# Layer 1 of a two-layer graph network: the block loop pipelined over three stages, with the edge-feature loads moved from SyncE to ScalarE

## What is computed

```python
h = relu(layernorm(x))
x = x + segment_sum(h[src], dst) @ W_rel.T + b_rel + h @ W_root.T      # layer 0
h = relu(layernorm(x))
w = silu(edge_attr_50 @ We1 + be1) @ We2 + be2                          # [200000, 128]
agg = segment_sum(h[src] * w, dst)                                      # layer 1
x = x + h + silu(agg @ Wn1 + bn1) @ Wn2 + bn2
```

## Time and profile before

| | us |
|---|---|
| median of 3 runs | 5581.96 |
| the profiled execution, whole | 5534.93 |
| its span, first to last instruction | 5533.1 |
| mean granted TensorE clock | 0.623 of full speed |
| POOL, PE, DVE, ACT busy | 54%, 46%, 36%, 21% |

### The profile page before, as it was taken

The page is one execution under the profiler, slowest core; times in us unless marked ns, Lnnn a source line. Parts: engine busy times, 40 slices in busy tenths (PEclk is TensorE's granted clock), DMA queues, the critical chain, the costliest instruction groups (busy, mean ns, idle before and its releaser), DMA issues.

```text
span 5533.1 us, 50710 instructions
## 1 busy us (share of the span) xinstructions
PE 2539.5 (46%) x10946; PEld 1935.5 (35%) x10946; DVE 1975.2 (36%) x6931; ACT 1188.8 (21%) x2730; POOL 2971.4 (54%) x3135
## 2 busy tenths in 40 slices
PE   1333333333333333342555555555555555554456
PEld 1323333333333333331333333444334433333334
DVE  3444444444444444451222332333333333222224
ACT  1333333333333333330010111111111111100001
POOL 6656666666666666625454454554444445445442
PEclk9555555555555555556666666666766666666667
DMA  2111111121211211211111121211111112111111
GB/s 66 51 52 51 51 53 50 52 54 49 56 50 49 55 51 50 57 40 48 51 52 50 50 54 51 54 53 49 51 49 51 51 49 54 51 51 52 51 51 47
DMA packets 205552, 284.71 MB, mean 51 GB/s; under 512 B 67808, under 2 KB 135442, under 8 KB 205298
## 3 DMA queue, kind: packets, MB, share of 16 engines
q0 software_dynamic: 100096, 205.20, 14.3%
q1 hardware_dynamic: 64146, 57.99, 3.9%
q10 hardware_dynamic: 41184, 20.45, 1.3%
HBM read 262.97 MB, written 20.45 MB: 51 GB/s over the span
## 4 chain that ended last, share of the span: by engine, by line
another core or an unknown queue 32%; PE 22%; DVE 20%; issue 19%; DVEq 4%; ACT 3%; DMA 0%; ACTq 0%; POOL 0%; SPq 0%; POOLq 0%
PE seg_a L315 9%; PE seg_b L315 5%; DVE onehot L552 5%; PE ew_ps L359 4%; DVE e_stats L568 3%; PE hid_ps L354 3%; DVE ew_ps L652 3%; DVEq L559 3%; DVE rows L656 2%; ACT rows L410 2%; DVE e_mv L572 2%; DVE agg L563 1%; DVE n_stats L585 1%; DVE e_rstd L577 1%
## 5 line engine op out<-in xcount | busy, mean ns | idle before, releaser
L283 POOL DMA_INDIRECT rows<-h_rows,idx x1564 | 1486.9, 951 | 1608.8 <-DMA idx<-src_cols 696.6
L283 POOL DMA_INDIRECT rows<-x,idx x1564 | 1483.5, 949 | 873.5 <-issue 469.1
L315 PE MATMUL seg_a<-onehot,rows 128*128 128x128 f32 x3312 | 751.4, 398 | 1519.4 <-ACT rows L410 454.8
L315 PEld LDWEIGHTS seg_a<-onehot,rows 128*128 128x128 f32 x3312 | 646.9, 290 | 1766.8 <-issue 1667.4
L315 PE MATMUL seg_b<-onehot,rows 128*128 128x128 f32 x2944 | 614.0, 374 | 1274.2 <-DVE rows L656 516.2
L315 PEld LDWEIGHTS seg_b<-onehot,rows 128*128 128x128 f32 x2944 | 528.9, 270 | 1493.0 <-issue 1298.8
L410 ACT ACTIVATE rows<-rows,e_shift,e_rstd 128x128 f32<-128x128 f32 x1564 | 643.2, 481 | 889.9 <-DVE e_shift L579 699.9
L488 ACT ACTIVATE hidden<-hid_ps,be_col 128x512 f32<-128x512 f32 x391 | 268.6, 687 | 2532.2 <-remote 1228.1
L359 PE MATMUL ew_ps<-we_sb,hidden 128*128 128x128 f32 x3128 | 564.2, 340 | 152.9 <-ACT hidden L488 111.7
L359 PEld LDWEIGHTS ew_ps<-we_sb,hidden 128*128 128x128 f32 x3128 | 524.7, 253 | 190.7 <-ACT hidden L488 142.4
L563 DVE TENSOR_TENSOR agg<-seg_b,agg 128x128 f32 x368 | 107.6, 292 | 1210.4 <-remote 812.6
(11 more groups left out here) (93 smaller groups left out, 898.2 us busy)
## 6 DMA issues: line engine op xcount, KB each, us to landing
rows<-x,idx POOLq DMA_INDIRECT x1564
rows<-h_rows,idx POOLq DMA_INDIRECT x1564
ef_a<-ef_blocks SPq DMA_DIRECT2D x69, 300.0 KB
ef_b<-ef_blocks SPq DMA_DIRECT2D x46, 300.0 KB
xs<-x SPq DMA_DIRECT2D x26, 256.0 KB
y_rows<-ys ACTq DMA_DIRECT2D x26, 256.0 KB
ys<-y_rows SPq DMA_DIRECT2D x26, 256.0 KB
out<-xs ACTq DMA_DIRECT2D x26, 256.0 KB
```

The lines of the kernel that those rows point to most:

```text
L283: pool.indirect_dma_start(out=rows[:, u, t, :], out_offset=None, in_=table, in_offset=bass.IndirectOffsetOnAxis(ap=idx[:, j:j + 1], axis=0 ...
L315: mm = pe.matmul(seg[u % 2][:, 0:P], rows[:, u, t, :], onehot[:, u % 2, t, :], start=(t == 0), stop=(t == TB - 1))
```

## The change

1. Layer 1's block loop is staggered. In step u PE does the first product of u + 2, the second product of u + 1, and the segment sum of u; DVE does the message of u, the one-hot of u + 1, the accumulation of u - 1 and the bias of u + 1. A prologue starts blocks 0 and 1, and at the end of each iteration the streams run on into the next one. After the last iteration two first products and one second product are left over and drained.
2. `hid_ps` and `ew_ps` get two banks each; `node_t` and `node_o` share one bank, for which PE waits (`hold` on `s_mout`) before the node update of layer 1. `onehot` gets three buffers; `hi_row` moves into a part of `agg[1]` to make room.
3. The edge-feature loads leave SP and go into ACT's stream: group g + 2 is issued after the silu of the last block of group g. SP's layer-1 program is then that of layer 0, with `ys` in place of `xs`.

```diff
 SyncE, layer 1
-                    for u in range(U):
-                        g, blocks = u // EF_BLOCKS, min(EF_BLOCKS, U - u)
-                        if u % EF_BLOCKS == 0:
-                            hold(sp, s_hid, done(i, u - EF_BLOCKS - 1) if g else done(i, EF_BLOCKS * (EF_GROUPS - 1) - 1 - U))
-                            sp.dma_start(ef[g % 2][:, 0:blocks, :],
...
-                        if u == HALF + EF_BLOCKS:
-                            for v in range(HALF):
-                                hold(sp, s_rows[1][v], i * (16 * TB) + 16 * TB)
-                            load_idx(it + 1, 0, HALF, s_idx_a)
+                    node_y([loop_group(it)], i)
+                    for u in range(HALF):
+                        hold(sp, s_rows[1][u], i * (16 * TB) + 16 * TB)
+                    load_idx(it + 1, 0, HALF, s_idx_a)
+                    for u in range(HALF, U):
+                        hold(sp, s_rows[1][u], i * (16 * TB) + 16 * TB)
                     load_idx(it + 1, HALF, U, s_idx_b)
 TensorE, layer 1
                 def hidden_layer():
+                    hold(pe, s_mout, n - r + 1)
                     hold(pe, s_acc[1], acc_done)
...
-                    edge_hidden(i, 0)
                     for u in range(U):
-                        edge_weights(i, u)
-                        if u + 1 < U:
-                            edge_hidden(i, u + 1)
                         if u in steps:
                             steps[u]()
-                        pe.wait_ge(s_msg, i * U + u + 1)
-                        segment_sum(1, i, u)
+                        if u + 2 < U:
+                            edge_hidden(i, u + 2)
+                            edge_weights(i, u + 1)
+                        elif u + 1 < U:
+                            edge_weights(i, u + 1)
+                            edge_hidden(i + 1, u + 2 - U)
+                        else:
+                            edge_hidden(i + 1, u + 2 - U)
+                        pe.wait_ge(s_msg, i * U + (u + 1))
+                        segment_sum(1, u)
+                        if u + 1 == U:
+                            edge_weights(i + 1, 0)
 ScalarE, layer 1
+            def load_ef(it, g):
+                first, last = g * EF_BLOCKS, min((g + 1) * EF_BLOCKS, U)
+                act.dma_start(ef[g % 2][:, 0:last - first, :],
...
                     for u in range(U):
-                        act.wait_ge(s_hid, done(i, u))
-                        act.wait_ge(s_ew, slot_free(i, u, 2))
...
+                        edge_silu(i, u)
+                        g = u // EF_BLOCKS
+                        if u == min((g + 1) * EF_BLOCKS, U) - 1:
+                            load_ef(it + (g + 2) // EF_GROUPS, (g + 2) % EF_GROUPS)
 VectorE, layer 1
+                    edge_bias(i, 0)
+                    one_hot(1, it, 0)
                     for u in range(U):
-                        one_hot(1, i, it, u)
                         message(i, u)
-                        add_window(1, i, it, u)
+                        if u + 1 < U:
+                            one_hot(1, it, u + 1)
+                        if u > 0:
+                            add_window(1, i, it, u - 1)
+                        if u + 1 < U:
+                            edge_bias(i, u + 1)
+                        else:
+                            add_window(1, i, it, u)
```

More of the change, by code:

```diff
@@ L29 @@
 EF_BLOCKS = 3
+HOT = 3
 EF_GROUPS = -(-U // EF_BLOCKS)
@@ L110, in build @@
         seg = [bank("seg_a"), bank("seg_b")]
-        hid_ps, ew_ps = bank("hid_ps"), bank("ew_ps")
-        node_t, node_o = [bank("node_t"), hid_ps, ew_ps], [bank("node_o"), *seg]
+        hid_ps, ew_ps = [bank("hid_a"), bank("hid_b")], [bank("ew_a"), bank("ew_b")]
+        node = bank("node")
+        node_t, node_o = [node, hid_ps[0], ew_ps[0]], [node, *seg]
         assert LATE <= 3
@@ L310, in _, with segment_sum @@
             pe.wait_ge(s_ident, 1)
[L312 to L313 removed]
+            def segment_sum(layer, u):
                 for t in range(TB):
[L315 removed]
+                    mm = pe.matmul(seg[u % 2][:, 0:P], rows[:, u, t, :], onehot[:, u % HOT, t, :],
                                    start=(t == 0), stop=(t == TB - 1))
@@ L479, in node_update1, with edge_silu @@
                 return {3: hidden_layer, 9: result, 14: stored}
+            def load_ef(it, g):
+                first, last = g * EF_BLOCKS, min((g + 1) * EF_BLOCKS, U)
+                act.dma_start(ef[g % 2][:, 0:last - first, :],
+                              ef_blocks[bass.ds(it * U + first, last - first)].rearrange("k c e -> c k e")
+                              ).then_inc(s_ef[g % 2], 16)
+            load_ef(0, 0)
+            load_ef(0, 1)
+            def edge_silu(i, u):
+                act.wait_ge(s_hid, i * U + (u + 1))
+                nc.scalar.activation(hidden[:, u % 2, :], hid_ps[u % 2][:, :], ACT.Silu,
+                                     bias=be1_col[:, :]).then_inc(s_silu, 1)
             with act.Fori(0, passes) as p:
@@ L485, in _ @@
                     for u in range(U):
-                        act.wait_ge(s_hid, done(i, u))
-                        act.wait_ge(s_ew, slot_free(i, u, 2))
-                        nc.scalar.activation(hidden[:, u % 2, :], hid_ps[:, :], ACT.Silu,
-                                             bias=be1_col[:, :]).then_inc(s_silu, 1)
+                        edge_silu(i, u)
+                        g = u // EF_BLOCKS
+                        if u == min((g + 1) * EF_BLOCKS, U) - 1:
+                            load_ef(it + (g + 2) // EF_GROUPS, (g + 2) % EF_GROUPS)
                         if u in steps:
                             steps[u]()
+            for g in range(2):
+                hold(act, s_ef[g], passes * (8 * EF_GROUPS * ITERS) + 16)
+            edge_silu(passes * ITERS, 0)
+            edge_silu(passes * ITERS, 1)
+            hold(act, s_ew, passes * ITERS * U + 1)
             with act.Fori(0, n_late) as j:
```

49 lines of the change are left out of this document (25 added, 24 removed).

## The result

The changed kernel takes 4950.97 us (median of 4 runs, 4927.46 to 4962.84); in the same session the kernel before takes 5581.93. The ratio is 0.8861, 95% interval 0.882 to 0.8903. Forecast were 4970 us and a range of 4785 to 5220. The profiled execution is one of 4927.46 us with a span of 4925.0 and a mean clock of 0.638.

A forecast was written before the change was run, and what follows sets the result against it. Bound: POOL's waits, 34.8 us per iteration for row indices. Start 2473, ring full 2573, pause to 2581, 371 blocks at 6.1 to 4844, tail to 4923; the 610 drop off the 5581.96 median gives 4970 us, range 4785 to 5220.

The forecast's parts named there:

- The wait for the index load goes: In layer 1, POOL's wait for the first half's row indices, 34.8 us per iteration, goes.
- Rival three: If node_y or the landing of rows comes late, POOL still waits up to 34.8 us: 5500 to 5600; chance 0.04.
- The pace at a full ring, 6.1 us per block: Layer 1 with gathering 17 blocks ahead takes 6.1 us per block, layer 0's value; bounds 5.0 and 7.0.
- The stagger worth nothing where POOL is the bound, and 7.0 without it: Layer 1's reordered block steps save nothing by themselves where POOL bounds; without them, 7.0 us per block.
- The late results: While gathers are issued without a pause, whoever needs a PE result gets it late, 11.2 us for one segment sum.
- rival one: Compute is never held up by gathers, POOL alone bounds at 5.0 us per block: about 4500; chance 0.08.
- The slow full ring (6.5 to 7.0): Layer 1 at a full ring is slower than layer 0, 6.5 to 7.0 us per block: 5120 to 5305; chance 0.20.
- Slower than before: Each layer 1 step pays one delay on top of PE's 6.05 us, 8.4 per block: 5825 in runs; chance 0.05.
- PE's hold, 0 to 3 us, taken as hidden: In step 2 PE waits until DVE accumulates block 1, 1 to 3 us per iteration, mostly hidden: put at 0.
- ACT's edge-feature loads, 0: Six edge-feature loads per iteration in ACT's stream, 2 to 4 us of issue: cost zero, at most 4.
- Layer 0 unchanged, the ends: Layer 0 loses no wait; layer 1's gathers start at 2460.26 as now and the 79 us tail stays.
- What the next profile would show: Signs: no index wait, iterations 102 to 106 us, POOL busy over 60%, waits 1 to 5 us, clock 0.6 to 0.8.

The follow-up runs named there:

- e1: Kernel before with only the edge-feature loads moved from SyncE to ScalarE; order of products, banks and one-hot buffers stay old: 5043.37 us, ratio 0.9021.
- e2: Changed kernel with the edge-feature loads back in SyncE's queue, ahead of the index load; stagger, banks and buffers kept: 5488.62 us, ratio 0.9833.
- e5: Changed kernel with layer 1's segment sum taking two of its four tiles per block: 4945.28 us, 103.7 us per iteration.
- e6: Changed kernel with layer 1's second product computed twice into the same bank: 5061.17 us, 107.9 us per iteration.
- e3: Changed kernel with layer 1's indirect gathers replaced by plain DMAs of 128 consecutive rows, still issued by POOL: 3887.66 us.
- e4: Changed kernel with layer 1's gathers replaced by plain DMAs of the same bytes issued by SyncE, index loads left out, POOL idle there: 3896.91 us.
- e10: Changed kernel with layer 1's gathers replaced by plain loads from POOL, each split into two of 64 rows: 4084.10 us, 69.55 us per iteration.
- e8: Changed kernel with PE's node-update hold asking for an accumulation two blocks earlier and ACT's two later update parts moved to steps 11 and 15: 4926.85 us, ratio 0.8799.
- e7: Changed kernel with one tiny POOL operation after each block's four gathers in layer 1: 4968.75 us, 104.0 us per iteration.
- e12: Changed kernel run again without alteration in the fourth session: 4905.37 us, ratio 0.8879 to the kernel before.
- e11: Changed kernel with POOL allowed only 8 blocks ahead in layer 1 in place of 17: 4884.14 us, 103.4 us per iteration.
- e9: Changed kernel with four small POOL operations after each block's gathers in layer 1, a real gap: 4904.86 us, 102.5 us per iteration.

## Why the prediction was right, step by step

**The wait for the index load goes.** Right in mechanism and size. It is shown from both sides: with the short queue alone (e1) the wait is gone and 543 us of time with it, of 631 for the whole change; without the short queue (e2) waits of 34 us remain. Rival three, the wait under another name, is out.

**The pace at a full ring, 6.1 us per block.** Measured 102.8/17 = 6.05. Taking it from layer 0 was right, and for a better reason than "most alike": e5 shows that the pace doesn't fall when PE has less to do (e6, with 8 records more per block, adds 4 to 5 us per iteration), and layer 0, with 8 matmuls per block in place of 18, runs at 102.7 to 104.9 us with the same gathers. 85 us of issue and 17 to 20 of stops are what 68 indirect gathers take in either layer.

**The stagger worth nothing where POOL is the bound, and 7.0 without it.** This step was mis-sized. Without it the pace is 107.4/17 = 6.32 (e1), not 7.0. The 7.0 was read from the pause that followed a run of 44 gathers, which the wait for indices itself had caused; at a steady full ring the runs are short and so are the pauses. The prediction had put some 330 us (371 x 0.9) on the stagger's presence; it is worth about 100 (4.6 us x 22, or 88 by the difference of the whole and e1), and about as much alone (e2, -98). The error didn't reach the sum, because both halves were in the change.

**The late results.** Seen in the profile and shown to be tied to the indirect gathers (e3, e4, e10). That reading kept the sum away from rival one. The Trainium skill's rule in SBUF — State Buffer, section "SBUF: two separate sides", that a DMA can't be slowed by a compute operation nor the other way round, agrees with e3 and e4 (114 GB/s beside a PE that is 94% busy). Read as "gathers cost compute nothing", it would give 85 us per iteration here, and layer 1 takes 102.8. Whether that goes against the rule itself isn't shown, since these runs don't part the transfer of an indirect gather from POOL's own work for it.

**Rivals.** POOL alone as the bound (85 us per iteration): out, with 17.6 us of pauses. The slow full ring (6.5 to 7.0): out for this kernel; e6 reaches 6.35 when PE has 8 matmuls more per block. Slower than before, from 7.75 us per block: not near, at 6.05. The 1.7 us of delay per step that it needed isn't there; that with three stages one late result holds up one of three products only is a reason that no run tests.

**PE's hold, 0 to 3 us, taken as hidden.** Its length was underrated: 89.0 us in 14 times from 2700 to 4700, up to 11.9 each. That it is mostly hidden was right: e8 takes it away, and of its 4.6 us per iteration 0.2 (POOL's waits) to 1.5 (the pace, against e7) come back.

**ACT's edge-feature loads, 0.** Nothing speaks against it, but no run measures it alone: e1, which has them, shows POOL waiting for segment sums and "remote" only, and its sum with e2 leaves 10 us for all that doesn't add.

**Layer 0 unchanged, the ends.** Gathers of layer 1 start at 2484.0, not at 2460, as layer 0 ran 1 us per iteration slower in that execution (in e12 they start at 2458.7). From the first to the end of the last gather it took 2367 us; the prediction's terms give 2384 (4844 - 2460). The tail is 4925.0 - 4850.6 = 74 us, said 79. So the span came out 2 us above the 4923 of the sum: +24 in layer 0, -17 and -5 behind it. That these cancel is luck; the size of each, under 1% of the span, is what the sum was good for. The 19 us by which 4970 is too high come from the distance of the profiled span to the median, 48.9 us before and 26.0 after: 23 us too much, less the 2 of the span and 2 of rounding.

**What the next profile would show.** Iterations of 102 to 106 us, POOL at 61%, a clock of 0.72 in layer 1: as said. Pauses were said to be 1 to 5 us; the mean is 2.3 beyond the regular 0.30, and three waits are longer, 6.4 to 7.8, each before the first gather of an iteration. PE's hold isn't their cause, as e8, without it, has three of 7.9 to 8.5 at the same place.

One reading of the prediction needs a correction. It lets the 12.55 us of the first gather of layer 1 fit the "DVE blocks DMA" box; the last section shows rows that don't fit.

Open: why results of PE come late beside indirect gathers (PE's ends are modelled, so a late result may also be one that PE finished later than its record says), why they are rarer in e1, and why POOL's free time is 17.5 to 19 us per iteration no matter where it lies.

## What to carry to other kernels

A load for the next iteration that stands in a queue behind a hold on this iteration's compute costs the whole lead that a deep ring was built for; look at what is issued a microsecond before the late load, and move the pacing holds to a queue of their own. Take the pace after the fix from a stretch that already runs in the new state, a sister loop for instance, and not from the recovery after the stall, which the stall itself made worse. Once the engine that issues the gathers is the bound, idle time of the others is worth little: taking away a hold of PE of 4.6 us per iteration (e8) gave 0.2 to 1.5. And look at the end: a deep ring leaves more blocks for the time after the last gather, 32 us more with 17 than with 8 (e11).

## What the runs showed of the hardware

- While POOL issues indirect gathers, results of PE reach DVE and ACT late against PE's records: by 10.2 us for the second product at 3611.58 in the changed kernel, and up to 35 in the earlier trace rows. Beside plain loads of the same bytes, from POOL without a pause (e10) or from SyncE (e4), DVE waiting for a segment sum uses it 0.13 to 0.14 us after its recorded end.
- 68 indirect gathers of 128 rows cost 85 us of issue and in the steady state 102.5 to 104.9 us in both layers. The median pause is near 1.0 + 0.15 us per gather of the run before it, from runs of 8 on, and the gap put in by hand was taken off the other stops (e9).
- A plain load from POOL takes 0.53 us of issue (2.12 for four, in e3), 0.51 in halves of 64 rows (e10); the gather takes 0.94 and 0.30 between.
- The first gather of layer 1 takes 12.55 us beside DVE's clearing of the accumulator (10.72 us), before and after. The same clearing in layer 0, from 13.85 to 24.57 in the changed kernel, has three gathers starting beside it that take 0.94 to 0.95 us each, and then one of 7.23; in e10 POOL's plain loads keep their pace beside it, ten in 5.22 us. The Trainium skill's "DVE blocks DMA" box in SBUF — State Buffer, section "SBUF: two separate sides", says that a DMA issued from POOL has to wait for its descriptors while DVE runs a two-port operation. The long gathers could be that, the short ones and e10's loads don't fit it, and no run shows whether the clearing is such an operation.
- The pace of layer 0 differs by 2% (102.7 to 104.9 us) between executions of the same code, and the medians of one kernel by 1.2% between sessions.
